# The low halves of the GELU tiles made on GpSimd, in a fused perceiver block

## What is computed

```python
x = x + xattn(layernorm(x), ctx, ctx, Wq, Wk, Wv, Wo, bo)
x = x + attn(layernorm(x), Wq, bq, Wk, bk, Wv, bv)      # causal, softmax over the whole matrix of a sequence
x = x + ffn(layernorm(x), w1, b1, w2, b2)
# ffn: gelu(x @ (mean|w1| * sign(w1)).T + b1) @ (mean|w2| * sign(w2)).T + b2, 512 -> 2048 -> 512
```

## Time and profile before

| engine | busy us | share of the span | instructions |
|---|---|---|---|
| PE | 2603.2 | 96% | 16820 |
| DVE | 1683.2 | 62% | 3520 |
| ACT | 1250.7 | 46% | 2766 |
| POOL | 776.1 | 28% | 1530 |

### The profile page before, as it was taken

The page is one execution under the profiler, slowest core; times in us unless marked ns, Lnnn a source line. Parts: engine busy times, 40 slices in busy tenths (PEclk is TensorE's granted clock), DMA queues, the critical chain, the costliest instruction groups (busy, mean ns, idle before and its releaser), DMA issues. The chain is left out here.

```text
span 2724.9 us, 51525 instructions
## 1 busy us (share of the span) xinstructions
PE 2603.2 (96%) x16820; PEld 1512.2 (55%) x16820; DVE 1683.2 (62%) x3520; ACT 1250.7 (46%) x2766; POOL 776.1 (28%) x1530
## 2 busy tenths in 40 slices
PE   7999999999999999999999999976899899989999
PEld 3555555555555555555555555533666566556666
DVE  7555656555555555555655565547676766766675
ACT  4345554445544454445444544423344444434444
POOL 2233433333333333333333333310211211111110
PEclk9999999999999999999999999987999999999999
DMA  4234433443333333333333333323000000000000
GB/s 143 99 84 106 104 90 90 97 98 82 82 86 92 83 82 85 89 88 82 82 89 90 82 82 87 70 68 116 16 16 17 31 15 15 31 15 15 16 24 16
DMA packets 344619, 187.76 MB, mean 69 GB/s; under 512 B 290672, under 2 KB 311152, under 8 KB 344048
## 3 DMA queue, kind: packets, MB, share of 16 engines
q1 hardware_dynamic: 344560, 187.00, 27.5%
HBM read 109.06 MB, written 8.65 MB: 43 GB/s over the span
## 5 line engine op out<-in xcount | busy, mean ns | idle before, releaser
L712 DVE TENSOR_TENSOR e_lo<-e,e_hi 128x1024 f16<-128x1024 f32 x128 | 156.8, 1225 | 413.9 <-ACT e_hi L640 413.9
L797 PE MATMUL psum<-c_hi,xWk_hi 128*128 128x512 f16 x1024 | 388.4, 379 | 2.3 <-PEq L140 2.3
L797 PE MATMUL psum<-xWv_hi,c_hi 128*128 128x512 f16 x1024 | 389.2, 380 | 0.0
L797 PE MATMUL psum<-xWv_lo,c_hi 128*128 128x512 f16 x1024 | 389.1, 380 | 0.0
L797 PE MATMUL psum<-xWv_hi,c_lo 128*128 128x512 f16 x1024 | 388.9, 380 | 0.0
L797 PE MATMUL psum<-c_lo,xWk_hi 128*128 128x512 f16 x1024 | 388.4, 379 | 0.0
L797 PE MATMUL psum<-c_hi,xWk_lo 128*128 128x512 f16 x1024 | 388.4, 379 | 0.0
L122 POOL TENSOR_TENSOR c_lo<-ctx_raw,c_hi 128x1024 f16<-128x1024 f32 x128 | 272.2, 2127 | 335.3 <-ACT c_hi L618 325.0
L633 ACT ACTIVATE e<-psum,neg_max 128x257 f32<-128x257 f32 x512 | 235.8, 474 | 280.8 <-DVE neg_max L693 280.8
L704 DVE SCALAR_TENSOR_TENSOR v_lo<-psum,v_hi 128x512 f16<-128x512 f32 x256 | 177.0, 691 | 249.8 <-ACT v_hi L626 249.8
L570 POOL COPY bd_hi<-heads_hi 32x128 f16 (+1 forms) x512 | 152.9, 299 | 575.4 <-PE psum L797 553.0
(11 more groups left out here) (224 smaller groups left out, 5586.8 us busy)
## 6 DMA issues: line engine op xcount, KB each, us to landing
ctx_raw<-in_ctx_main SPq DMA_DIRECT2D x128, 512.0 KB, 3.6
xs<-in_x SPq DMA_DIRECT2D x8, 1024.0 KB, 5.7
v_rep<-v_last_rows SPq DMA_DIRECT2D x512, 16.0 KB, 1.7
xb<-in_x SPq DMA_DIRECT2D x16, 512.0 KB, 3.4
out<-res_out SPq DMA_DIRECT2D x32, 256.0 KB, 2.1
ffn_raw<-in_w_t SPq DMA_DIRECT2D x11, 512.0 KB, 3.4
late_raw<-in_late_w SPq DMA_DIRECT2D x4, 1024.0 KB, 4.8
res<-in_w_t SPq DMA_DIRECT2D x5, 512.0 KB, 3.6
```

The lines of the kernel that those rows point to most:

```text
L712: nc.vector.tensor_tensor(e_lo[:, :, :], e[:, :, 0:S], e_hi[:, :, :], ALU.subtract).then_inc(e_lo_done, 1)
L797: mm = nc.tensor.matmul(bank, a, b, start=(n == 0), stop=(n == len(steps) - 1))
```

## The change

POOL makes the low halves of the GELU tiles with the same subtraction that DVE made, and DVE's `hidden` goes. POOL's other work of the round is put between the steps: the power for norm 2 between F(0) and F(1), the copy of `at_hi` behind F(1), the copy of `at_lo` behind F(3), the input's two tiles behind F(6) and F(8), now one instruction each, the power for norm 3 behind F(12), and b2's two tiles, one instruction each, behind F(14) and F(15). The semaphores `xb_done` and `b2_added` count tiles instead of groups.

```diff
-            def stage_input(n):
+            def stage_input(n, *tiles):
                 pool.wait_ge(s["x_landed"], 16 * (n + 1))
-                nc.gpsimd.tensor_tensor(xb[:, :, :], xb[:, :, :],
-                                        bo_row[:, :].unsqueeze(1).to_broadcast([P, T, D]),
-                                        ALU.add).then_inc(s["xb_done"], 1)
+                for t in tiles:
+                    nc.gpsimd.tensor_tensor(xb[:, t, :], xb[:, t, :], bo_row[:, :],
+                                            ALU.add).then_inc(s["xb_done"], 1)
+
+            def hidden(g, j):
+                pool.wait_ge(s["gelu_hi_done"], NJ * g + j + 1)
+                nc.gpsimd.tensor_tensor(act_lo[j % AR][:, :], act[j % AR][:, :], act_hi[j % AR][:, :],
+                                        ALU.subtract).then_inc(s["gelu_lo_done"], 1)
+
+            def add_b2(n, u, t):
+                pool.wait_ge(s["norm3_done"], T * n + t + 1)
+                nc.gpsimd.tensor_tensor(res[u][:, t, :], res[u][:, t, :], b2_row[:, :],
+                                        ALU.add).then_inc(s["b2_added"], 1)
...
             def one(n, u, front, ffn):
-                if not front:
-                    return
-                power(n, s["eps2_done"], s["rstd2_done"])
-                if not (isinstance(n, int) and n == NG - 1):
-                    stage_heads(n + 1)
-                    stage_input(n + 1)
-                power(n, s["eps3_done"], s["rstd3_done"])
-                pool.wait_ge(s["norm3_done"], T * (n + 1))
-                nc.gpsimd.tensor_tensor(res[u][:, :, :], res[u][:, :, :], ...
+                F(0)
+                if front: power(n, s["eps2_done"], s["rstd2_done"])
+                F(1)
+                if following: stage_heads(n + 1, (heads_hi, at_hi))
+                F(2, 3)
+                if following: stage_heads(n + 1, (heads_lo, at_lo))
+                F(4, 5, 6)
+                if following: stage_input(n + 1, 0)
+                F(7, 8)
+                if following: stage_input(n + 1, 1)
+                F(9, 10, 11, 12)
+                if front: power(n, s["eps3_done"], s["rstd3_done"])
+                F(13, 14)
+                if front: add_b2(n, u, 0)
+                F(15)
+                if front: add_b2(n, u, 1)
...
         # in DVE's list
-            def hidden(g, j):
-                dve.wait_ge(s["gelu_hi_done"], NJ * g + j + 1)
-                nc.vector.tensor_tensor(act_lo[j % AR][:, :], act[j % AR][:, :], act_hi[j % AR][:, :],
-                                        ALU.subtract).then_inc(s["gelu_lo_done"], 1)
...
-                dve.wait_ge(s["b2_added"], g + 1)
+                dve.wait_ge(s["b2_added"], T * (g + 1))
...
-                    dve.wait_ge(s["xb_done"], n + 1)
+                    dve.wait_ge(s["xb_done"], T * (n + 1))
```

More of the change, by code:

```diff
@@ L1084, in _, with stage_heads @@
         def _(pool):
-            def stage_heads(n):
+            def stage_heads(n, *which):
                 pool.wait_ge(s["wo_ps"], T * n)
-                for src, dst in ((heads_hi, at_hi), (heads_lo, at_lo)):
+                for src, dst in which:
                     nc.gpsimd.tensor_copy(dst[:, :, :], src[:, :, bass.ds(n * GROUP, GROUP)]
                                           ).then_inc(s["at_done"], 1)
-            def stage_input(n):
+            def stage_input(n, *tiles):
                 pool.wait_ge(s["x_landed"], 16 * (n + 1))
-                nc.gpsimd.tensor_tensor(xb[:, :, :], xb[:, :, :],
-                                        bo_row[:, :].unsqueeze(1).to_broadcast([P, T, D]),
-                                        ALU.add).then_inc(s["xb_done"], 1)
+                for t in tiles:
[9 more added lines that the diff above has]
+                                        ALU.add).then_inc(s["b2_added"], 1)
             def power(n, eps_done, rstd_done):
@@ L1103, in one, with F @@
             def one(n, u, front, ffn):
-                if not front:
-                    return
-                power(n, s["eps2_done"], s["rstd2_done"])
-                if not (isinstance(n, int) and n == NG - 1):
-                    stage_heads(n + 1)
-                    stage_input(n + 1)
-                power(n, s["eps3_done"], s["rstd3_done"])
-                pool.wait_ge(s["norm3_done"], T * (n + 1))
-                nc.gpsimd.tensor_tensor(res[u][:, :, :], res[u][:, :, :],
-                                        b2_row[:, :].unsqueeze(1).to_broadcast([P, T, D]),
-                                        ALU.add).then_inc(s["b2_added"], 1)
+                g = n - 1
+                following = front and not (isinstance(n, int) and n == NG - 1)
+                def F(*js):
+                    for j in js:
+                        if ffn:
+                            hidden(g, j)
+                F(0)
+                if front:
+                    power(n, s["eps2_done"], s["rstd2_done"])
+                F(1)
+                if following:
+                    stage_heads(n + 1, (heads_hi, at_hi))
+                F(2, 3)
+                if following:
+                    stage_heads(n + 1, (heads_lo, at_lo))
+                F(4, 5, 6)
+                if following:
+                    stage_input(n + 1, 0)
+                F(7, 8)
+                if following:
+                    stage_input(n + 1, 1)
+                F(9, 10, 11, 12)
+                if front:
+                    power(n, s["eps3_done"], s["rstd3_done"])
+                F(13, 14)
+                if front:
+                    add_b2(n, u, 0)
+                F(15)
+                if front:
+                    add_b2(n, u, 1)
             nc.gpsimd.memset(half[:, :], -0.5).then_inc(s["pool_const"], 1)
             pool.wait_ge(s["consts_landed"], 16 * 6)
-            stage_input(0)
+            stage_input(0, *range(T))
             nc.gpsimd.memset(zeros[:, :], 0.0).then_inc(s["pool_const"], 1)
@@ L1121, in _ @@
             pool.wait_ge(s["pool_const"], 4)
-            pool.wait_ge(s["xb_done"], 1)
+            pool.wait_ge(s["xb_done"], T)
             for b in range(BPT):
@@ L1389, in F @@
                     for j in js:
-                        if ffn:
-                            hidden(g, j)
-                        else:
+                        if not ffn:
                             for piece_nr in SPLIT_SLOTS.get(j, ()):
```

## The result

The changed kernel takes 2664.32 us (median of four, 2663.45 to 2664.69) against 2729.86 us (2727.81 to 2732.71) for the kernel before: a ratio of 0.9759, 95% interval 0.9742 to 0.9776, 65.5 us less. The forecast was 2673 us in a range of 2660 to 2702.

What follows compares the result with a forecast made beforehand. PE, busy 96% of the span, was held by waits for GELU low halves and slow clock behind them. From 2726.66 us, 43.8 + 15.2 - 0.7 = 58 us less gave 2669, on the median's scale 2673 us, range 2660 to 2702.

Steps and rivals of the forecast that it cites:

- The bound and its cause: PE waits twice a round for GELU low halves, 55.7 us in all; DVE and POOL exclude each other on a port.
- The price of the subtraction: One 128x256 subtraction on POOL takes 0.67 us, within bounds of 405 and 1153 ns.
- The rival that had it at twice VectorE's: POOL's subtraction costs 0.85 us, making layer 2 of early steps later: 5 us, 2678 us in all; chance 0.09.
- The round's start: Layer 2 of step 2 starts 3.13 us earlier in each of 14 rounds, with three short PE waits left.
- The rest of the round: Later steps, norm 3, b2 and attention move nothing PE waits for; low halves need at most 1.96 of 2.27 us.
- The attention chain: DVE's scores, weights and values before PE's weighted sum; as a rival, lost slack costs 17 us, 2690 us; chance 0.13.
- The worst case: Attention, every two-input DVE instruction and cast caught behind POOL: values ready at 2255.95, 0.3 us before the weighted sum.
- The slow clock: PE's slow matmuls behind the 3.58 us stall go, gaining 15.2 us; rival that they stay: 2688 us, chance 0.07.
- The signs: Expected profile after: POOL's and DVE's busy times, PE's waits, clock and 49.0 us rounds, plus three signs of being wrong.
- The sum: Against the profiled 2726.66 us: 43.8 + 15.2 - 0.7 = 58 us less, so 2669 us.
- The term that missed most: The 4.3 us by which the profiled execution lay under the median of three, taking 2669 to 2673 us.
- The rival on the other side: POOL can't keep the steps' pace: 2.13 us a subtraction gives 2784 us, deciding from about 1.85; chance 0.05.

Runs made afterwards that it cites:

- e1: Kernel before, with POOL's head copies and input addition made to wait for step 5's high half, DVE keeping all low halves: 2661.75 us, ratio 0.9753.
- e2: Kernel before, with step 2's low half moved ahead of normalise for norm 2 in DVE's list: 2685.18 us, ratio 0.9842.
- e5: Changed kernel, with each GELU subtraction on POOL twice as wide (128x512): 2696.54 us, ratio 0.9881.
- e6: Changed kernel, with each GELU subtraction on POOL three times as wide (128x768): 2755.82 us, ratio 1.0097.
- e3: Changed kernel, with head copies and both input tiles in one block behind the power, ahead of step 1's low half: 2750.79 us, ratio 1.0081.

## Why the prediction was right

**The bound and its cause**: right. The two waits a round were the place, and e1 shows the collision with POOL's pieces as the cause of the long one: take them away and DVE's instructions have their own durations. e2 shows the same from the other side.

**The price of the subtraction**: 0.667 us from a line through the 128x512 and 128x1024 rows, measured 0.671 (median of 256, 0.661 to 1.208). The rival that had it at twice VectorE's is out, and with it that ratio of the Trainium skill ("GPSIMD Engine Reference", section "Engine selection") for this size: 0.671 to 0.424 is 1.6. The argument for that rival, that on wide tiles POOL is no faster than twice VectorE's time, was wrong as well: on 128x1024, POOL takes 2127 ns and VectorE 1225, a ratio of 1.7.

```profile
L712 DVE TENSOR_TENSOR e_lo<-e,e_hi x128: 1224/1225/1226, 148.9 to 1802.0; 128x1024 f16<-128x1024 f32 x128
```

That the subtraction is slower on POOL is right. At this price it was hidden but for the round's start; e5 shows that twice the width is not.

**The round's start**: the waits were forecast as 0.16, 0.65 and 0.23 us by the distance of starts, 1.04 in all; measured 0.33, 0.47 and 0.23, 1.03. That the sum fits to 0.01 is luck, since the first two are off by 0.17 and 0.18 us in opposite directions. The first is higher in part because I counted 0.05 us from POOL's end to PE's start, where this one took 0.14 (2246.72 to 2246.86); the second is lower mostly because the power took 0.71 us, not 0.85. The power of 0.85 us had a subtraction on DVE beside it, and so had e1's:

```profile
2276.76 0.43 DVE L1211 TENSOR_TENSOR gelu_lo<-gelu,gelu_hi 128x256 f16<-128x256 f32 x1
```

The gain a round was 3.28 us, forecast 3.13.

**The rest of the round**: right. The attention chain was caught as feared, at the cast and the subtraction of the second tile of values (1.29 and 1.04 us for 0.43 and 0.69), and had slack: `val_lo` is ready at 2226.35, PE begins the weighted sum at 2227.88, 1.53 us later, where it was 2.62 before. The worst case, with 0.3 us left, did not come.

```profile
2223.99 1.29 DVE L1330 CAST val_hi<-val 128x512 f16<-128x512 f32 x1
2225.31 1.04 DVE L1332 TENSOR_TENSOR val_lo<-val,val_hi 128x512 f16<-128x512 f32 x1
```

**The slow clock**: its 15.2 us went, as forecast; the rounds after are all at 1.00.

**The signs**: two came out otherwise. DVE's busy time was to fall by more than the 159 us of its subtractions, since blocked time would go with them; it fell by 107, because the rest of DVE's work was caught more. And a POOL subtraction over 0.85 us was to be a sign of being wrong: the longest took 1.208 us and the mean is 0.723, since some are caught behind DVE. An undisturbed one costs what was forecast, so this sign was badly chosen and does not speak against the price. The others held: POOL 184 us more (forecast 171), PE's waits some 14 us in all by the distance of starts (forecast 15; the list has 5.4 of them), rounds of 48.84 us (forecast 49.0).

**The sum**: 58 us forecast against the profiled execution, 62.2 measured (2726.66 to 2664.5). 14 x 0.15 = 2.1 of the 4 are the round's start. From one round's first layer-1 matmul to the next, the first three rounds take 49.38, 48.64 and 48.64 us, the first of them 53.44 before; these and the fourteenth (48.63) gave some 1.4 us more. And from round 15's first layer-1 matmul to the end of the span nothing was lost (77.5 before, 77.2 after), where I had 0.7. There I had overlooked a wait: before, step 15's low half was caught behind the b2 addition of 2.47 us, and PE waited for it in the last round, 0.65 us by the distance of starts.

```profile
2688.54 1.96 DVE L1211 TENSOR_TENSOR gelu_lo<-gelu,gelu_hi 128x256 f16<-128x256 f32 x1 [0.53 <-ACT gelu_hi L1144]
2690.56 0.39 PE L1492 MATMUL psum<-shared,gelu_hi 128*128 128x512 f16 x1 [0.49 <-DVE gelu_lo L1211]
```

The other way went 0.7 us before the first round. **The term that missed most** is the last of the sum: I added 4.3 us to come from the profiled execution to the median of the runs. The kernel before spreads over 5 to 8 us from run to run, the changed one over 1.2 (2663.45 to 2664.69), and its profiled execution lies at the median. The spread of the former goes with the slow stretches, 8 rounds in that execution and by their clocks not as many in each: of all its runs on record, the ten under 2729.3 us have a mean granted clock of 0.983 to 0.985, the twelve above 2730.7 one of 0.981 to 0.983. With the slow stretches gone, so is the spread, and the 4.3 us with it. That the runs differ in their slow rounds is read from the clock alone; the rounds were counted in one execution. Without the 4.3 the forecast would have been 2669, and 5 us off.

**The rival on the other side**: its mechanism is real, its turning point was wrong. I had it at 1.85 us per subtraction. Between e5 (1.16, 33 us faster than before) and e6 (1.65, 27 slower) a straight line crosses at 1.43. The step that failed is mainly the slack of the later steps, taken one by one against a single undisturbed piece: the pieces and the subtractions also catch DVE and are caught by it, and the norm's chain on DVE is lengthened by them. In e6 that is 2.1 of the 2.9 us a round that the working was short; the other 0.8 are at the round's start.

## What to carry to other kernels

Before moving work off an engine that seems late, look at what stretches its instructions: a duration of several times the median beside a long instruction of the neighbour (here VectorE and GpSimd) is the sign of a collision, and moving the long one to a quiet stretch may be worth as much as moving the work. When an in-order queue gets new work with a deadline, put the pieces without a deadline behind it and waits for others' results (here the power) behind whatever is ready sooner. Read PE's waiting time from the distance of starts: the list of waits showed 0.30 us where 0.70 were to be had. And before calling an engine needed for a gain, try the other order of the list that is there.

## What the runs showed of the hardware

- PE's clock fell from 2.4 to 1.2 GHz behind a wait of 3.58 us in 8 of 14 rounds (kernel before), and in e3 at the end of all 14 waits of 4.2 to 5.1 us, where the first matmul was already slow (0.51 to 0.61 us). With the waits of up to 0.4 us in each round of the changed kernel, up to 1.0 of e2, up to 0.7 of e5, and up to 1.25 in e6's rounds 2 to 14 the granted clock stayed at 1.00. It fell once in e6 at 1906 us, behind two waits of 1.1 us that came 2 us apart, and at 2702 us behind the one of 2.99: a short wait is harmless mostly, not always.
- The exclusion works both ways and lets the engines take turns: POOL's 128x1024 copy of 1.03 us took 1.23 when a `normalise` tile was in progress, and DVE's cast of 0.43 us took 1.29 beside an input tile. The rule for it in the Trainium skill ("SBUF — State Buffer", section "Who interferes with whom") agrees with both. The loser's loss is nearly what is left of the winner's instruction: the cast asked at 2223.99, the input tile ran until 2224.99, and the cast lost 0.86 us.
